# Layer 3's routing: the lane comparison on GpSimd as two 128-column comparisons

## What is computed

```python
scores = xf @ gate_w + gate_b
gate_probs = jax.nn.sigmoid(scores)
gate_logits = scores + expert_biases
_, topk_idx = jax.lax.top_k(gate_logits, K)          # K = 2 of E = 8 experts
top_k_probs = jnp.take_along_axis(gate_probs, topk_idx, axis=-1)
top_k_probs = top_k_probs / top_k_probs.sum(axis=-1, keepdims=True)
...
for e in range(E):
    h = jax.nn.relu(xf @ w1[e] + b1[e])
    out = out + combine[:, e:e + 1] * (h @ w2[e] + b2[e])
```

## Time and profile before

| what | value |
| --- | --- |
| median of three executions | 2414.94 us (2412.57 to 2416.8) |
| profiled execution, first to last instruction (its span) | 2414.8 us |
| PE busy | 2096.5 us (87%) |
| DVE busy | 1678.3 us (69%) |
| ACT busy | 1283.7 us (53%) |
| GpSimd busy | 711.2 us (29%) |

### The profile page before, as it was taken

The page is one execution under the profiler, slowest core; times in us unless marked ns, Lnnn a source line. Parts: engine busy times, 40 slices in busy tenths (PEclk is TensorE's granted clock), DMA queues, the critical chain, the costliest instruction groups (busy, mean ns, idle before and its releaser), DMA issues. The chain is left out here.

```text
span 2414.8 us, 45217 instructions
## 1 busy us (share of the span) xinstructions
PE 2096.5 (87%) x15328; PEld 1597.7 (66%) x15328; DVE 1678.3 (69%) x3514; ACT 1283.7 (53%) x2221; POOL 711.2 (29%) x688
## 2 busy tenths in 40 slices
PE   5969777999987899959998467999985499999998
PEld 4758533444445788859998223444454399999998
DVE  2867756888845776636665697888835877777775
ACT  2434443666653444235554233666652088888885
POOL 1423200222220000038887000222210045555553
PEclk7989887999998899969999786999997799999999
DMA  3000033212103000086665342212104367777774
GB/s 123 1 0 0 0 84 101 59 51 56 51 9 108 3 1 1 1 198 117 116 98 70 102 106 75 59 50 56 51 1 110 123 207 220 222 222 223 222 224 97
DMA packets 176774, 218.56 MB, mean 91 GB/s; under 512 B 34057, under 2 KB 152498, under 8 KB 176242
## 3 DMA queue, kind: packets, MB, share of 16 engines
q1 hardware_dynamic: 146290, 175.19, 23.6%
q0 software_dynamic: 30336, 41.44, 10.7%
HBM read 161.25 MB, written 54.79 MB: 89 GB/s over the span
## 5 line engine op out<-in xcount | busy, mean ns | idle before, releaser
L1403 ACT ACTIVATE L_attn_probs<-L_attn_ps_t 128x512 f32<-128x512 f32 x640 | 374.8, 598 | 245.1 <-PE L_attn_ps_t L1327 240.0
L1310 PE MATMUL L_attn_ps_m<-L_attn_k,L_attn_q 96*128 96x512 bf16 (+3 forms) x1024 | 283.4, 316 | 35.3 <-DMA L_attn_k<-L_k_parts 28.7
L1273 POOL TENSOR_SCALAR_AFFINE_SELECT L_attn_probs<-L_attn_probs 128x512 f32<-128x512 f32 x256 | 153.3, 635 | 469.0 <-ACT L_attn_probs L1403 469.0
L1310 PEld LDWEIGHTS L_attn_ps_m<-L_attn_k,L_attn_q 96*128 96x128 bf16 x1024 | 101.8, 99 | 240.6 <-issue 71.8
L1327 PE MATMUL L_attn_ps_t<-L_attn_q,L_attn_k 98*128 98x512 bf16 (+3 forms) x1024 | 245.0, 301 | 2.8 <-ACT L_attn_probs L1403 2.3
L2450 POOL DMA_INDIRECT out<-L_experts_result,L_moe_give x78 | 161.7, 2073 | 208.6 <-DVE L_experts_result L2622 196.8
L1443 DVE TENSOR_REDUCE L_attn_top<-L_attn_ps_m 128x1 f32<-128x512 f32 x256 | 175.3, 685 | 61.8 <-PE L_attn_ps_m L1312 60.6
L1312 PE MATMUL L_attn_ps_m<-L_attn_causal,L_attn_ident 128*128 128x128 bf16 x1024 | 200.6, 227 | 0.0
L1348 PE MATMUL L_attn_ps_v<-L_attn_probs,L_attn_v 128*32 128x512 f32 (+3 forms) x2048 | 191.4, 448 | 3.0 <-POOL L_attn_probs L1273 2.8
L2729 POOL DMA_INDIRECT L_experts_token<-L_moe_rows,L_moe_take x80 | 81.8, 1022 | 377.7 <-POOLq L1766 324.0
L2468 PE MATMUL L_experts_ps_y<-L_experts_w_high,L_experts_hT_low 128*128 128x256 f32 x624 | 179.5, 288 | 0.0
(11 more groups left out here) (435 smaller groups left out, 6110.5 us busy)
## 6 DMA issues: line engine op xcount, KB each, us to landing
L_staged_w<-L_ffn_w SPq DMA_DIRECT2D x78, 1024.0 KB, 6.6
L_attn_q<-L_q_parts SPq DMA_DIRECT2D x64, 192.0 KB
L_attn_q<-L_q_parts SPq DMA_DIRECT2D x64, 128.0 KB
L_moe_rows<-L_moe_ln_normed SPq DMA_DIRECT2D x16, 512.0 KB, 3.0
L_q_parts<-L_qkv_q_parts SPq DMA_DIRECT2D x32, 192.0 KB, 2.9
L_q_parts<-L_qkv_parts SPq DMA_DIRECT2D x32, 192.0 KB, 3.1
load_ring<-x SPq DMA_DIRECT2D x8, 512.0 KB, 4.2
L_attn_q<-L_q_parts SPq DMA_DIRECT2D x64, 64.0 KB
```

The costliest lines, as they stand in the source:

```text
L1273: return pool.affine_select(out=block, in_=block, compare_op=ALU.is_ge, fill=0.0, base=0, pattern=columns, channel_multiplier=-1)
L1310: pe.matmul(bank[:, at:at + width], q[j][0:96, head, qb * P:(qb + 1) * P], k[j][0:96, 0:width], start=True, stop=False)
L1403: act.activation(probs[j % 2][:, place[unit], :], ps_t[:, n % 2, :], ACT.Exp, scale=scale).then_inc(exped, 1)
```

## The change

The comparison that makes `lanes` leaves DVE in layer 3 and is made by GpSimd, as one comparison of 128 columns for each choice with `low` as a scalar per partition. GpSimd begins when `low` is there (`lanes_asked`), which is now copied before `high`; it waits for `sides_used` as DVE does, and PE waits for `lanes_ready` beside `sides_ready`. GpSimd's 32 tiles are written out, without a loop. In layer 2 the comparison stays where it was; there the first tile gets a wait for `lanes_asked`.

```diff
+        lanes_asked, lanes_ready = sem("lanes_asked"), sem("lanes_ready")
...
                     pe.wait_ge(sides_ready, t + 1)
+                    if shared is None:
+                        pe.wait_ge(lanes_ready, t + 1)
...
+            if shared is None:
+                @block.gpsimd
+                def _(pool):
+                    def lanes_of(t, p, first_):
+                        if not first_:
+                            pool.wait_ge(sides_used, t - 1)
+                        for c in range(2):
+                            last = pool.tensor_scalar(lanes[p][:, c, :], lane[:, :], low[:, c, t:t + 1], None,
+                                                      ALU.is_equal)
+                        last.then_inc(lanes_ready, 1)
+                    constants.wait(pool)
+                    pool.wait_ge(lanes_asked, 1)
+                    for t in range(NT):
+                        lanes_of(t, t % 2, t < 2)
...
+                    dve.tensor_copy(low[:, :, :], low_i[:, :, :]).then_inc(lanes_asked, 1)
                     did(dve.tensor_copy(high[:, :, :], high_i[:, :, :]))
-                    did(dve.tensor_copy(low[:, :, :], low_i[:, :, :]))
...
-                    dve.tensor_tensor(lanes[p], lane[:, :].unsqueeze(1).to_broadcast(by_lane),
-                                      low[:, :, ds(t, 1)].to_broadcast(by_lane), ALU.is_equal)
+                    if shared is not None:
+                        if t == 0:
+                            dve.wait_ge(lanes_asked, 1)
+                        dve.tensor_tensor(lanes[p], lane[:, :].unsqueeze(1).to_broadcast(by_lane),
+                                          low[:, :, ds(t, 1)].to_broadcast(by_lane), ALU.is_equal)
```

## The result

The changed kernel took 2433.47 us (median of 6 runs, 2425.69 to 2437.37), the kernel before 2416.8 us beside it (median of 6, 2412.57 to 2420.73). The ratio taken over all runs is 1.0064, 95% interval 1.0049 to 1.008; by the medians it is slower by 16.7 us, where +2.65 us was forecast and 2432.0 was the upper end of the range. A comparison takes 0.60 us in odd tiles and 0.74 in even ones, both above the 0.46 us with which the forecast's own sum ended, and PE never reached its upper clock in the loop.

What follows compares the result with a forecast made beforehand. The prediction took layer 3's table loop to be bound by its ring of two buffers, 2.04 us a turn. A turn of 2.20 gave 15 x 0.16 = 2.4, and +0.25 made +2.65 us: 2417.5 us, range 2411.5 to 2432.

Steps and rivals of the forecast that it cites:

- The ring of two buffers: Layer 3's table loop: PE uses a buffer, DVE refills it, PE uses it again; 2.04 us a turn of two tiles.
- DVE loses the comparison: Table loop: `valued` would start 0.36 us after `hits` in place of 0.57; at most 3.4 us gained.
- GpSimd gains 64 comparisons: Table loop: each comparison of 128 columns taken as 0.37 us, between 0.29 and 0.46.
- rival A: Table loop: a comparison costs GpSimd more than 0.46 us; at 0.60, +12 us, 2427 us; chance 0.28.
- the turn-taking: Table loop: DVE and GpSimd take strict turns at reading SBUF; a turn of the ring 2.09 us, against 2.04.
- A's signs: In the table loop: GpSimd back to back, PE released by it each time, `valued` done earlier.
- The two engines collide: Table loop: DVE's `hits` and `valued` and GpSimd's comparison, all reading SBUF, take turns; 2.09 us a turn, 0.07 added for pushing.
- a hold: Time a GpSimd comparison needs after DVE's release: 0.14 us less than its record, 0.23 for one of 0.37.
- Rival D: Table loop: neither engine begins under the other's drain, whole records add up; turn 2.52 us, +7, 2422 us; chance 0.07.
- Rival C: Table loop: a longer ring leaves PE idle, its clock falls back; 0.61 us more a turn, +12, 2426 us; chance 0.03.
- The start: Ahead of the first tile: perhaps two of four comparisons delay DVE, less 0.21 saved; +0.25 us, between -0.21 and +0.7.
- PE's additional wait: Table loop: one more semaphore for PE to pass per tile; 0.04 us a turn, bounds 0 to 0.06.

## Why the prediction was wrong

- *What bounds the kernel*: right. The ring of two buffers set the pace, and the loop's loss came through (15.0 of the 16.6 us between the two spans; behind the loop the two differ by 0.25). With four buffers and DVE alone, PE's pace fell to DVE's 0.96.
- *DVE loses the comparison*: `valued` starts 0.36 behind `hits` for the first tile (1888.98 to 1889.34) as worked out, but 0.45 in the loop (1909.81 to 1910.26); before, with the comparison between them, the distance was 0.57 in both places, so the 0.09 could not be seen. It mattered for nothing, as GpSimd was late.
- *GpSimd gains 64 comparisons*: this is the first step that failed. I took 0.37 us, between a line through one-input rows and a line through two-input rows, and gave 0.46 as the far end; it is 0.60 by itself. A line through a copy and a mask says nothing of a tensor with a scalar: 2.5 ns a column against 0.89, more even than two tensors. That was rival A's record to the hundredth, though there 0.60 stood as an example and not as a forecast, and A was then priced by the turn-taking, and not by GpSimd's own throughput, which the runs show: 4 x 0.58 = 2.31 us a turn (one SBUF input, upper clock). Of A's signs PE released by GpSimd and `valued` done earlier came true; GpSimd back to back did not, as it idles 0.46 us a turn.
- *The two engines collide*: right in kind, wrong in size and side. I let a hold be the record less 0.14, which made DVE wait. In the trace GpSimd's records stretch (0.60 to 0.74) and DVE's hardly do (487 against 476 ns). With the clock held it is worth 2.46 - 2.31 = 0.15 us a turn, at the lower clock 3.06 - 2.80 = 0.26. Rival D, whole records in turns, falls: `hits` runs in the middle of a comparison and keeps its 0.32.
- *Rival C, the clock*, got a chance of 0.03, on the argument that gaps grow only to 0.3 us a tile. That argument used the forecast's comparison. With the real one PE waited 0.53 us in every turn at the lower clock, and never left it. It is the largest part: 3.06 - 2.46 = 0.60 us a turn, by the run in which PE's gaps were filled.
- The sum of a turn: 2.04 before; +0.27 for GpSimd's throughput, +0.15 for collisions, +0.60 for the clock, is 3.06. The parts are for this order; taken away first, the collision alone is worth more, since the clock then rose by itself. Times 15: 4.0 + 2.3 + 9.0 = 15.3, measured 15.0: the 15 turns grew by 14.2 only, since two of them had been at the lower clock before, and the last two tiles behind them took 0.8 more. The failing of the method was to price A and C as alternatives, 12 us each. The dear comparison, with its collision, kept the clock down: with the collision gone, and the comparison at 0.60, it rose after 11.6 us. Together A and C went beyond the range.
- *The start*: +0.25 forecast, -0.06 measured; beside the first four comparisons DVE needed 0.15 us more from line 2124 to `hits` (2.75, before 2.60), where 0.46 was taken, and the 0.21 saved was as forecast.
- *PE's additional wait*: PE starts 0.15 behind GpSimd's end, against 0.06 behind DVE's before; 0.09 a turn where 0.04 was taken. Whether that is the wait or GpSimd's signal stays open.

## What to carry to other kernels

Before an operation is moved to GpSimd, measure that very operation there in its shape: a row of a neighbouring kind can be off by a factor of two (288 ns for a copy, 600 for the comparison), and here the fixed part of one comparison alone (0.28 us) exceeds what DVE's refill got shorter by in the loop (0.12 us, 0.57 less 0.45). In a ring of two buffers a slower refill also makes PE wait, and a PE that waits may stay at half its clock, so price the slow case with the lower clock's durations too, and not the clock as a rival of its own. Where the ring is the bound, more buffers are a first thing to try: in one run they took 10.1 of the loop's 15.0 us back with the comparison still on GpSimd.

## What was not expected of the hardware

A comparison and a multiplication of a tensor with a scalar cost GpSimd the same, and more (600 ns for 128 columns) than a subtraction of two tensors (398 in two of three records). The collision falls on GpSimd, by 0.14 us (in the changed kernel in even tiles alone), where in the earlier trace rows DVE lost 0.9 us beside GpSimd's two-input subtraction. And PE's clock has two outcomes for nearly the same loop: at 2.80 us a turn it rose after 11.6 us, at 3.06 it never did, and when it had been brought up ahead of the loop it fell after two tiles; with four buffers it rose once and held while PE was busy 21.33 of 34.00 us.
